# A job's sixteen mix units: twelve in three fp32r passes and four in fp32, with an arena of 460 cells

## The reference

```python
q = x @ Wq + bq          # 16 columns
k = x @ Wk + bk
v = x @ Wv + bv          # 128 columns
attn = softmax(einsum('bnd,bmd->bnm', q, k), axis=-1)   # 1024 x 1024 for each picture
out = gamma * einsum('bnm,bmc->bnc', attn, v) + x       # gamma in the first of the two alone
```

## Time and profile before

| | us |
|---|---|
| median of three runs | 4506.18 (4506.09 to 4507.4) |
| profiled execution, its own time | 4507.79 |
| its span, first to last instruction | 4505.7 |
| mean granted clock of TensorE | 0.99 |
| busy: PE, DVE, ACT, POOL | 4346, 3473, 2841, 2263 |
| attention stage, first to last cast | 811.8 to 3794.0 |

### The profile page before, as it was taken

The page is one execution under the profiler, slowest core; times in us unless marked ns, Lnnn a source line. Parts: engine busy times, 40 slices in busy tenths (PEclk is TensorE's granted clock), DMA queues, the critical chain, the costliest instruction groups (busy, mean ns, idle before and its releaser), DMA issues.

```text
span 4505.7 us, 56695 instructions
## 1 busy us (share of the span) xinstructions
PE 4346.3 (96%) x16776; PEld 2251.6 (50%) x16776; DVE 3472.9 (77%) x6544; ACT 2840.7 (63%) x5241; POOL 2262.9 (50%) x3972
## 2 busy tenths in 40 slices
PE   6989996999999999999999999999999999999998
PEld 2446654444444444444444444444444444445755
DVE  5988876777777777777777777777777775898877
ACT  1323322788888888888888888888888885233322
POOL 4655321455555555555555555555555556564432
PEclk9999997899999999999999999999999999999999
DMA  6668429111111122222221111111222221124211
GB/s 188 74 69 109 95 28 67 41 60 60 55 56 58 60 69 72 67 65 70 71 70 56 55 58 60 60 60 61 66 70 72 72 67 45 64 88 119 67 56 47
DMA packets 314722, 309.72 MB, mean 69 GB/s; under 512 B 253744, under 2 KB 257328, under 8 KB 309296
## 3 DMA queue, kind: packets, MB, share of 16 engines
q1 hardware_dynamic: 311312, 305.06, 27.5%
q10 hardware_dynamic: 3104, 1.06, 0.1%
HBM read 137.21 MB, written 135.27 MB: 60 GB/s over the span
## 4 chain that ended last, share of the span: by engine, by line
PE 66%; DVE 9%; ACT 8%; issue 8%; POOL 7%; DMA 1%; SPq 0%; DVEq 0%; ACTq 0%; POOLq 0%
PE psum L1179 14%; PE psum L1097 8%; PE psum L1087 6%; PE psum L1150 6%; PE psum L1111 5%; POOL probs_low L616 4%; PE psum L1163 3%; PE psum L1187 3%; PE psum L1185 3%; PE psum L1184 3%; PE psum L1222 3%; PE psum L1209 3%; PE psum L1200 3%; PE psum L1106 3%; ACT shared L992 3%
## 5 line engine op out<-in xcount | busy, mean ns | idle before, releaser
L616 POOL TENSOR_TENSOR probs_low<-shared,probs_high 128x512 fp32r<-128x512 f32 x1024 | 1307.2, 1277 | 1300.1 <-DVE probs_high L927 1300.1
L889 DVE TENSOR_REDUCE top<-psum 128x1 f32<-128x1024 f32 x1024 | 1253.9, 1225 | 616.3 <-PE psum L1163 616.0
L997 ACT ACTIVATE psum<-psum,top 128x1024 f32<-128x1024 f32 x1024 | 1114.2, 1088 | 282.0 <-DVE top L889 282.0
L992 ACT ACTIVATE shared<-psum 128x512 f32<-128x512 f32 x2048 | 1107.2, 594 | 258.9 <-PE psum L1150 258.9
L1179 PE MATMUL psum<-shared 128*128 128x512 f32 x2048 | 1123.0, 630 | 0.9 <-issue 0.5
L982 ACT ACTIVATE shared<-psum,b_col 128x320 f32<-128x320 f32 (+10 forms) x744 | 413.2, 566 | 995.9 <-PE psum L1097 981.1
L607 POOL TENSOR_TENSOR shared<-arena 128x32 f32<-128x32 f32 (+6 forms) x1230 | 584.4, 505 | 764.5 <-PE psum L1097 753.5
L1184 PE MATMUL psum<-probs_high,v_high 128*128 128x512 f32 x1024 | 811.1, 792 | 0.0
L1087 PE MATMUL psum<-arena,w_own 128*128 128x320 f32 (+12 forms) x1672 | 539.7, 450 | 35.0 <-DVE w_own L702 34.1
L1097 PE MATMUL psum<-shared,w_sum 128*128 128x320 f32 (+10 forms) x1488 | 519.5, 471 | 17.1 <-DVE shared L837 10.8
L1150 PE MATMUL psum<-q,k 64*128 64x512 f32 x2048 | 513.3, 497 | 0.3 <-ACT shared L992 0.3
(11 more groups left out here) (114 smaller groups left out, 4455.9 us busy)
## 6 DMA issues: line engine op xcount, KB each, us to landing
layer_out<-x SPq DMA_DIRECT2D x128, 512.0 KB, 2.6
x<-layer_out SPq DMA_DIRECT2D x124, 512.0 KB, 3.2
q<-q SPq DMA_DIRECT2D x256, 128.0 KB, 2.3
arena<-x_cells SPq DMA_DIRECT2D x6, 1520.0 KB, 7.0
layer_out<-arena SPq DMA_DIRECT2D x6, 1520.0 KB, 19.8
arena<-layer_out SPq DMA_DIRECT2D x6, 1520.0 KB, 10.6
y_cells<-arena SPq DMA_DIRECT2D x6, 1520.0 KB, 6.4
arena<-x_cells SPq DMA_DIRECT2D x4, 1504.0 KB, 27.9
```

What stands on the lines that cost most here:

```text
L616: nc.gpsimd.tensor_tensor(probs_low[n % 2][:], probs[u % PROBS], probs_high[n % 2][:], ALU.subtract).then_inc(probs_split, 1)
L889: nc.vector.reduce_max(top[i % 2][:, m:m + 1], rows_ps[m % 2][:], AX_X, negate=True).then_inc(row_max, 1)
L992: nc.scalar.activation(probs[u % PROBS], keys_ps[u % 2], ACT.Exp).then_inc(probs_ready, 1)
L997: nc.scalar.activation(rows_ps[m % 2][:], rows_ps[m % 2][:], ACT.Exp, bias=top[i % 2][:, m:m + 1], accum_out=total[i % 2][:, m:m + 1]).the ...
```

## The change

- Units with u % 4 != 3 are mixed in three passes (`in_passes`), twelve of a job; units 3, 7, 11 and 15 in fp32. `split_count` numbers the split ones.
- `probs_high` and `probs_low` get four buffers each. `mixed` now counts split units, a new semaphore `whole_mixed` the fp32 ones.
- PE's order: an odd slot takes the first two passes of its two units and the last pass of the first; the last pass of the second comes in the next slot. An even slot takes the fp32 unit, that pass, and then the three passes of its split unit. An fp32 unit no longer opens the sum in `mix_ps`.
- DVE casts, and POOL splits, two units in even slots and one in odd slots.
- The values: two tiles stay whole (`v`) and six are split. ACT has three copies (256, 256 and 512 columns) where it had two of 512, DVE two `low_values` (256 columns in slot 2, 512 in slot 4, both before the row maximum) where it had one of 512 in slot 3.
- `CHUNK` 96 to 80 and `WINDOW` 452 to 400: 16 chunks where there were 14, an arena of 460 cells where it had 512. Eight chunks are still loaded without a tenant before them. Chunk 7 is now asked for after level 13 and first read at level 22; before, chunk 7 was asked for at 13 and chunk 8 at 26.

```diff
-CHUNK = 96
+CHUNK = 80
-WINDOW = 452
+WINDOW = 400
...
+SPLITS = UNITS * 3 // 4
...
+def in_passes(u):
+    return u % 4 != 3
+def split_count(i, u):
+    return SPLITS * i + 3 * (u // 4) + u % 4
+WHOLE_TILES = [5, 7]
+SPLIT_TILES = [0, 4, 1, 2, 6, 3]
+SPLIT_PART = [slice(0, 2 * P), slice(2 * P, 6 * P)]
+RAW_PART = [slice(2 * P, 4 * P), slice(0, 4 * P)]
...
             for s in range(MT):
-                split_probs(j, 2 * s + 1)
+                for u in (2 * s, 2 * s + 1):
+                    if in_passes(u):
+                        split_probs(j, u)
                 if s == 2:
                     log_sums(j + 1)
                 if s == 3:
                     shift_values(j + 1)
...
-                positive(dve, mixed, 2 * (n - 2) + 2)
-                nc.vector.tensor_copy(probs_high[n % 2][:], probs[u % PROBS]).then_inc(probs_rounded, 1)
+                positive(dve, mixed, n - PROBS + 1)
+                nc.vector.tensor_copy(probs_high[n % PROBS][:], probs[u % PROBS]).then_inc(probs_rounded, 1)
...
+            if s in (2, 4):
+                low_values(j + 1, s // 4)
             row_maximum(j + 1 + (s + 6) // MT, (s + 6) % MT)
...
-            if s == 3:
-                low_values(j + 1)
...
-            round_probs(j, 2 * s + 1)
+            for u in (2 * s, 2 * s + 1):
+                if in_passes(u):
+                    round_probs(j, u)
...
-                if u % 2 == 0:
-                    positive(act, mixed, UNITS * i + u - PROBS + 1)
+                if in_passes(u):
+                    positive(act, probs_split, split_count(i, u) - 2)
                 else:
-                    positive(act, probs_split, UNITS // 2 * i + u // 2 - PROBS // 2 + 1)
+                    positive(act, whole_mixed, UNITS // 4 * i + u // 4)
...
+        def mix_high(i, u):
+            if is_job(i):
+                n = split_count(i, u)
+                if u == 0:
+                    pe.wait_ge(v_ready, 3 * i + 3)
+                if u % MT == 0:
+                    positive(pe, out_ready, 2 * i + u // MT)
+                pe.wait_ge(probs_rounded, n + 1)
+                nc.tensor.matmul(mix_ps, v_high[i % 2][:, split_rows(u)], probs_high[n % PROBS][:],
+                                 start=(u % MT == 0), stop=False)
+                nc.tensor.matmul(mix_ps, v_low[i % 2][:, split_rows(u)], probs_high[n % PROBS][:],
+                                 start=False, stop=False)
+        def mix_low(i, u):
+            if is_job(i):
+                n = split_count(i, u)
+                pe.wait_ge(probs_split, n + 1)
+                nc.tensor.matmul(mix_ps, v_high[i % 2][:, split_rows(u)], probs_low[n % PROBS][:],
+                                 start=False, stop=(u % MT == MT - 2)).then_inc(mixed, 1)
+        def mix_whole(i, u):
+            if is_job(i):
                 pe.wait_ge(probs_ready, UNITS * i + u + 1)
...
+                nc.tensor.matmul(mix_ps, v[i % 2][:, tile(u % MT // 4)], probs[u % PROBS], start=False, stop=False
+                                 ).then_inc(whole_mixed, 1)
...
-            for u in (2 * s - 2, 2 * s - 1):
-                mix(j + u // UNITS, u % UNITS)
+            i, u = j + (2 * s - 2) // UNITS, (2 * s - 2) % UNITS
+            if s % 2 == 1:
+                mix_high(i, u)
+                mix_high(i, u + 1)
+                mix_low(i, u)
+            else:
+                mix_whole(i, u + 1)
+                mix_low(i, u - 1)
+                mix_high(i, u)
+                mix_low(i, u)
```

More of the change, by code:

```diff
@@ L313, in tile, with value_tiles @@
     return slice(m * P, (m + 1) * P)
+def in_passes(u):
[6 more added lines that the diff above has]
+RAW_PART = [slice(2 * P, 4 * P), slice(0, 4 * P)]
+def value_tiles(h):
+    return WHOLE_TILES + SPLIT_TILES[:2] if h == 0 else SPLIT_TILES[2:]
 def queries_at(g, h):
@@ L360, in network @@
     k = [sb(f"k{n}", [P, BANK], F32R) for n in range(DEEP)]
[L361 to L365, removed]
+    v = [shared[n][:, 0:P * len(WHOLE_TILES)] for n in range(2)]
+    v_high = [sb(f"v_high{n}", [P, P * len(SPLIT_TILES)], F32R) for n in range(2)]
+    v_low = [sb(f"v_low{n}", [P, P * len(SPLIT_TILES)], F32R) for n in range(2)]
+    probs_high = [sb(f"probs_high{n}", [P, BANK], F32R) for n in range(PROBS)]
+    probs_low = [sb(f"probs_low{n}", [P, BANK], F32R) for n in range(PROBS)]
     probs = [shared[2 + n // 2][:, half(n % 2)] for n in range(PROBS)]
@@ L423, in network @@
     keys_ready, probs_ready, mixed, out_ready = (sem(n) for n in ("keys_ready", "probs_ready", "mixed", "out_ready"))
+    whole_mixed = sem("whole_mixed")
     block = ctx.enter_context(nc.Block())
@@ L613, in split_probs @@
             if is_job(i):
[L614 removed]
+                n = split_count(i, u)
                 pool.wait_ge(probs_rounded, n + 1)
[L616 removed]
+                nc.gpsimd.tensor_tensor(probs_low[n % PROBS][:], probs[u % PROBS], probs_high[n % PROBS][:], ALU.subtract
                                         ).then_inc(probs_split, 1)
@@ L666, in _ @@
                     shift_values(j + 1)
-        pool.wait_ge(mixed, UNITS * JOBS)
+        pool.wait_ge(mixed, SPLITS * JOBS)
         scan(1)
@@ L923, in round_probs, with low_values @@
             if is_job(i):
-                n = UNITS // 2 * i + u // 2
+                n = split_count(i, u)
                 dve.wait_ge(probs_ready, UNITS * i + u + 1)
-                positive(dve, mixed, 2 * (n - 2) + 2)
-                nc.vector.tensor_copy(probs_high[n % 2][:], probs[u % PROBS]).then_inc(probs_rounded, 1)
-        def low_values(i):
+                positive(dve, mixed, n - PROBS + 1)
+                nc.vector.tensor_copy(probs_high[n % PROBS][:], probs[u % PROBS]).then_inc(probs_rounded, 1)
+        def low_values(i, h):
             if is_job(i):
-                dve.wait_ge(v_rounded, i + 1)
-                nc.vector.tensor_tensor(v_low[i % 2][:], misc_ps, v_high[i % 2][:], ALU.subtract
+                dve.wait_ge(v_rounded, 2 * i + h + 1)
+                part, raw = SPLIT_PART[h], RAW_PART[h]
+                nc.vector.tensor_tensor(v_low[i % 2][:, part], misc_ps[:, raw], v_high[i % 2][:, part], ALU.subtract
                                         ).then_inc(v_ready, 1)
@@ L944, in output @@
             if is_job(i):
-                dve.wait_ge(mixed, UNITS * i + MT * (h + 1))
+                dve.wait_ge(mixed, SPLITS * i + SPLITS // 2 * (h + 1))
                 nc.vector.scalar_tensor_tensor(x[i % DEEP][:, half(h)], mix_ps, bv_col[job_layer(i)][:],
@@ L972, in _ @@
                 attention(j, s)
-        dve.wait_ge(mixed, UNITS * JOBS)
+        dve.wait_ge(mixed, SPLITS * JOBS)
         scan(1)
@@ L1003, in values @@
                 if h == 0:
-                    nc.scalar.activation(v[i % 2], misc_ps, ACT.Copy).then_inc(v_ready, 1)
-                else:
-                    nc.scalar.activation(v_high[i % 2][:], misc_ps, ACT.Copy).then_inc(v_rounded, 1)
+                    nc.scalar.activation(v[i % 2], misc_ps[:, 0:P * len(WHOLE_TILES)], ACT.Copy).then_inc(v_ready, 1)
+                nc.scalar.activation(v_high[i % 2][:, SPLIT_PART[h]], misc_ps[:, RAW_PART[h]], ACT.Copy
+                                     ).then_inc(v_rounded, 1)
         def shrink_sums(i):
@@ L1072, in _ @@
         fill_last_picture()
-        act.wait_ge(mixed, UNITS * JOBS)
+        act.wait_ge(mixed, SPLITS * JOBS)
         for lv in range(LEVELS):
@@ L1166, in row_energies, with split_rows @@
             mm.then_inc(rows_ready, 1)
[L1168 to L1177, removed]
-                pe.wait_ge(probs_ready, UNITS * i + u + 1)
[L1179 to L1188, removed]
+        def split_rows(u):
+            return tile(3 * (u % MT // 4) + u % 4)
@@ new lines, in mix_low @@
+        def mix_low(i, u):
+            if is_job(i):
+                n = split_count(i, u)
+                pe.wait_ge(probs_split, n + 1)
[3 more added lines that the diff above has]
+            if is_job(i):
+                pe.wait_ge(probs_ready, UNITS * i + u + 1)
+                nc.tensor.matmul(mix_ps, v[i % 2][:, tile(u % MT // 4)], probs[u % PROBS], start=False, stop=False
+                                 ).then_inc(whole_mixed, 1)
@@ L1219, in project_values @@
             else:
-                pe.wait_ge(v_ready, 2 * i + 1)
-            for m in range(MT // 2):
-                mm = nc.tensor.matmul(misc_ps[:, tile(m)], x[i % DEEP][:, tile(h * MT // 2 + m)],
+                pe.wait_ge(v_ready, 3 * i + 2)
+            for m, at in enumerate(value_tiles(h)):
+                mm = nc.tensor.matmul(misc_ps[:, tile(m)], x[i % DEEP][:, tile(at)],
                                       wv_sb[job_layer(i)][:], start=True, stop=True)
@@ L1230, in turn_shift @@
             pe.wait_ge(shift_ready, i + 1)
-            pe.wait_ge(v_ready, 2 * i + 2)
+            pe.wait_ge(v_ready, 3 * i + 3)
             nc.tensor.matmul(misc_ps[0:2 * MT, 0:P], shift[i % 2][:], ident_r[:], start=True, stop=True
```

## The result

The changed kernel takes 4565.75 us (median of four runs, 4564.72 to 4569.03) against 4506.14 us: 1.0133 times, 95% interval 1.012 to 1.0146, so 60 us slower. The profiled execution has a span of 4564.0 us where the one before had 4505.7.

The account below looks back on a forecast made before the run. PE was taken as the bound, with the DVE-POOL line level from slot 2 to slot 5. Period 23.10 us plus delay 1.05 gives 24.15 against 23.38: +0.77 x 127.6 = +98 us, 4604 us; range 4475 to 4675, likeliest 4560 to 4655.

Parts of the forecast that it names:

- PE's sum: PE's matmul work per job: 0.64 us less, plus the 0.13 wait gone, giving 22.6 us if PE alone set the pace.
- The line: DVE and POOL work from slot 2's row energies to turn_shift: split 4 starts at A + 1.80, shift ready at A + 8.62.
- A: The end of the row energies of slot 2 on PE, from which the forecast counts times; 2009.46 us in the old trace.
- The rest of PE's job after `mix_low(8)`: PE's work from behind that pass in slot 5 to the next job's slot 2 row energies, put at 12.92 us.
- The delay c: Time POOL's line loses because casts and POOL operations exclude each other: 1.05 us a job, between 0.75 and 1.4.
- cast 5 before split 4: Slot 2: cast 5, right behind cast 4, is running when split 4 wants to start, making it 0.24 to 0.4 us late.
- cast 6: Asked for after slot 3's maximum while split 5 runs; it goes next, making log_sums 0.2 to 0.3 us late.
- casts 8 and 9: Asked for after slot 4's maximum, during split 6; they go ahead of or between shift_values' small operations, costing 0.3 to 0.7 us.
- Casts that slip in for free: Rival: casts don't hold POOL up, PE waits 0.57 us, period 23.10 us, 4470 us; chance 0.13 for faster.
- PE with its whole gain: Rival: POOL's line is shorter than reckoned, so PE gets its whole 0.64 us a job: 4424 us; chance 0.06.
- DVE as the bound: Rival: casts wait for a split each time, DVE needs 24.8 us a job, +185 us, 4691 us; chance 0.13.
- The arena: Smaller chunks and window cost nothing, since chunk loads are covered; a late chunk would cost 10 to 30 us once.

Follow-up runs that it names:

- Experiment 2: Changed kernel with POOL subtracting only 8 of 512 columns for four of a job's twelve splits, output incomplete: 4418.02 us, 0.9801 times the kernel before.
- experiment 3: Changed kernel with all twelve roundings a job written as a reduction (tensor_reduce) in place of a cast: 4579.16 us, 1.0157 times the kernel before.
- experiment 4: Changed kernel with the rounding as a reduction for units 5, 6, 8 and 9 alone, the others casts: 4492.89 us, 0.9963 times the kernel before.
- experiment 9: Changed kernel with POOL's subtraction for unit 6 done twice, in slot 3: 4817.83 us, 1.0685 times the kernel before.
- experiment 10: Changed kernel with POOL's subtraction for unit 10 done twice, in slot 5: 4615.01 us, 1.0235 times the kernel before.
- experiment 5: Changed kernel with fp32 units 5 and 7 of each eight in place of 3 and 7: 4462.42 us, 0.9899 times the kernel before.
- experiment 7: Changed kernel with fp32 units 5 and 7 of each eight, and the rounding of units 2, 3 and 6 as a reduction: 4424.92 us, 0.9813 times the kernel before.
- experiment 8: Changed kernel with the last pass of an odd slot's second unit put back in that slot: 4817.13 us, 1.0683 times the kernel before.
- experiment 6: Changed kernel with fp32 units 5 and 7, reductions for units 4, 6, 8, 9, and DVE's guess behind slot 2's rounding: 4493.21 us, 0.9963 times the kernel before.

## Why the forecast was right, and where it was off

- **PE's sum.** -0.64 and the wait of 0.13 gone, 22.6 us. Experiment 2 has 22.70. The 0.43 of the pass behind the query projection (2022.66 above) confirms that 0.20 goes with the change of tile shape: no fp32 work starts there any more, and the 0.20 is still paid. The Trainium skill's page "TensorEngine Tiling (Array Packing)" (Key Properties) says that a change of the tiling mode drains the engine; these rows agree with it.
- **The line.** Split 4 at A + 1.80: exact. The line undisturbed, from there to the shift, 6.82 us: experiment 3 has 6.82 to `turn_shift`, experiment 4 6.79. The rest of PE's job after `mix_low(8)`, 12.92: measured 23.87 + 6.38 - 17.34 = 12.91. Experiments 9 and 10 show that place decides, 5 and 7 that the line can be cleared.
- **A reading that was wrong.** The prediction has the line of the kernel before go over DVE and POOL alone and calls it level with PE. Between 2010.86 and 2013.68 that chain is on ACT and behind its copy of the values (rows above), so POOL's line was not yet the limit then. The sum wasn't hurt, because it was built from POOL's own steps and because the change moves `v_low` away from there. That ACT doesn't hold the new line up came out so, but the prediction doesn't show it.
- **The delay c** is the term that was mis-sized: the time and the mechanism came out as forecast, this size did not. Forecast 1.05 (0.75 to 1.4); `mix_low(8)` came at A + 10.48 where 9.95 + c was written, so c was 0.53. By its parts: cast 5 before split 4 0.14 (split 4 started on time, but splits 4 and 5 took 2.60 to the next start, not 2.46; forecast 0.24 to 0.4), cast 6 0.13 (`log_sums` 1.69, not 1.56; forecast 0.2 to 0.3), casts 8 and 9 0.21 (`shift_values` 1.78, not 1.57; forecast 0.3 to 0.7). Each is about half or less of what was written. L665 grew by 0.46, but the next operation started 0.38 behind L665's start (2013.72 to 2014.10) where before it was 0.19 (2016.03 to 2016.22), only 0.19 later: in the records a small POOL operation overlaps the next one's start, and I had added the casts' lengths in full.
- **What was missing** is the other way: a pass for which PE had to wait costs 0.48 and not 0.23. 9.95 + 0.53 + 0.25 + 13.15 = 23.88, the measured period. Forecast 24.15, so 0.28 x 127.6 = 36 us too many. The first jobs, forecast to move by 3 us at most, came out 5.4 us shorter, and the mean job took 23.89 and not 23.87, which is 2 to 3 us the other way. Together that is the 38 us between 4604 and 4566. That two errors, c too large by 0.52 and the dearer pass left out (0.25), half cancel is luck.
- **PE's waits.** 0.3, 1.0 and 0.2 a job were forecast before `mix_low(6)`, at `turn_shift` and before `mix_low(8)`, 1.5 together. In PE's timeline these start 0.55, 1.02 and 0.37 behind the instruction before, where a stream has 0.23, 0.33 and 0.23: 0.32, 0.69 and 0.14 late, 1.15 together. The period is 1.17 over that of experiment 2.
- **The rivals.** Casts that slip in for free (4470 us) fell with the mean cast of 579 ns and with L665; experiments 3 and 4 price the exclusion at 0.57 to 0.60 us a job, just what separates slower from faster here. PE with its whole gain (4424) needs POOL's line cleared, which experiments 2 and 7 did, each at that time within 7 us. DVE as the bound (4691; its own sum gives 1.42 and not 1.45 us, 4687) didn't happen in this kernel, which leaves DVE 2.77 us idle a job with its blocked time counted as busy; in experiment 3 DVE became a part of the chain. The Trainium skill, "SBUF — State Buffer", Who interferes with whom, says that a cast can contend with GpSimd and that a reduction on this chip never does. Experiments 3 and 4 agree: L665, 0.69 beside casts 8 and 9, is 0.23 beside reductions, and two splits in a row 2.52 in place of 2.64.
- **The arena** was put at nothing, and alone it gives some 5 us with an interval that nearly reaches nothing. Its trace has 2.8 of 4.4 us behind the last cast (708.9 us to the end where the kernel before has 711.7); the changed kernel has 711.3 there, so it doesn't show that gain.

Left open: why the clock falls in some jobs of experiments 8 and 9 and not in others with the same waits of PE; which part of the change makes the first jobs 5.4 us shorter; and whether the parts of c would be the same for casts that begin at another point of a split.

## What to carry to other kernels

When an engine at 96% is made faster, look for the places where the chain of waits leaves it: what another line of engines needs between two such places is the next bound, however idle those engines are on average, and a microsecond there can cost several times what it costs elsewhere (1.26 against 0.35 us a job in experiments 9 and 10). Before more casts and more GpSimd subtractions are put next to each other, count who will be running when each is asked for; the slower form that takes no part in the exclusion paid where GpSimd was on the line (experiment 4) and lost where VectorE was (3 and 6). Moving work off such a line works only if it doesn't come back at its head.

## What the runs showed of the hardware that was not expected

- A TensorE pass that had to wait costs 0.20 to 0.28 us more in the chain than one in a stream (0.43 to 0.51 against 0.23). The ends of these records are modelled. By starts alone, the next instruction follows `mix_low(8)` after 0.43 us where 0.32 is usual; the rest is the overlap with the pass before, which is lost.
- In experiment 9 PE idled for 1.53 us before one pass and 0.48 before another, and then its instructions took up to twice their time: row energies 0.43, the key projection 1.52 in place of 1.01. The mean clock is 0.96 over each stretch of 500 us from 1000 to 3500, but it is not every job: 63 of 109 periods have a fall and 46 have none, and the job of 2040.41 stays at 1.00 behind the same two waits (1.53 and 0.48). In experiment 8 16 of 109 have one, the job of 1029.14 behind waits of 0.62 and 0.90. The changed kernel shows none: all 117 periods in that stretch round to 23.9. The timeline of experiment 9 around the waits, and a row of its chain behind them:

```profile
2012.34 0.51 PE L1224 MATMUL psum<-probs_low,v_high 128*128 128x512 f32 x1 [1.53 <-POOL probs_low L644]
...
2013.98 0.23 PE L1276 MATMUL psum<-ident_r,shift 128*16 128x128 f32 x1 [0.48 <-POOL shift L680]
```

```profile
2017.17 1.52 PE psum L1244 x4
```

- A cast that waits for a running subtraction of GpSimd seems to get its turn before GpSimd's next instruction, though that is already in the queue. Cast 6 ends at 2011.11 and L648, whose record starts at 2010.78, only at 2011.17; in the view by source, L648's median over 128 jobs is 389 ns, its shortest 201. The order is read from these lengths, not seen.
